# The top-4 choice of a mixture of experts moved into the attention ahead of it, with the experts' up weights loaded during that attention's last quads

## The reference, cut to what matters

```python
H, NH, NOPE, ROPE, VD, E, I, TOPK = 256, 16, 128, 64, 128, 16, 176, 4
SHI = I * 2
hid = hidden_states + attn_out
x2 = rmsnorm(hid, ln2_w).reshape(-1, h)
logits = x2 @ gate_w.T
probs = jax.nn.softmax(logits, axis=-1)
top_w, top_i = jax.lax.top_k(probs, TOPK)
top_w = top_w / jnp.sum(top_w, axis=-1, keepdims=True)
gu = jnp.einsum('th,eih->tei', x2, w1)          # g, u = its two halves
act = jax.nn.silu(g) * u
down = jnp.einsum('tei,ehi->teh', act, w2)
routed = jnp.einsum('te,teh->th', wfull, down)  # wfull: top_w at the chosen experts
shared = jax.nn.silu(sg) * su @ sh_down_w.T     # sg, su = halves of x2 @ sh_gu_w.T
return hid + (routed + shared).reshape(b, s, h)
```

## Time and profile before

| what | value |
|---|---|
| runs | 2027.96, 2036.36, 2041.23 us; median 2036.36 |
| profiled execution | 2040.3 us, its span 2038.6 us |
| TensorE busy | 1617.7 us (79%) |
| VectorE busy | 1374.7 us (67%) |
| ScalarE busy | 819.6 us (40%) |
| GpSimd busy | 600.5 us (29%) |
| mean granted TensorE clock | 0.901 of full |

### The profile page before, as it was taken

The page is one execution under the profiler, slowest core; times in us unless marked ns, Lnnn a source line. Parts: engine busy times, 40 slices in busy tenths (PEclk is TensorE's granted clock), DMA queues, the critical chain, the costliest instruction groups (busy, mean ns, idle before and its releaser), DMA issues. The chain is left out here.

```text
span 2038.6 us, 29782 instructions
## 1 busy us (share of the span) xinstructions
PE 1617.7 (79%) x9318; PEld 1137.7 (56%) x9318; DVE 1374.7 (67%) x3796; ACT 819.6 (40%) x2363; POOL 600.5 (29%) x720
## 2 busy tenths in 40 slices
PE   3559998788253888889889499999954999698883
PEld 2424443355121566666666388888842555588872
DVE  6679969588794888888888435555355333368875
ACT  2113444376231666666667223333310222144551
POOL 0020002167303877787777210000025000311000
PEclk9679999889576999999999799999966999799996
DMA  1305520100665600000000500000062222523100
GB/s 62 109 0 172 184 88 1 66 13 1 28 133 199 212 1 1 2 1 1 1 1 1 175 23 1 15 1 1 1 205 85 76 89 76 209 94 106 60 32 11
DMA packets 104406, 129.33 MB, mean 63 GB/s; under 512 B 14208, under 2 KB 89185, under 8 KB 101057
## 3 DMA queue, kind: packets, MB, share of 16 engines
q1 hardware_dynamic: 95264, 112.39, 17.2%
q0 software_dynamic: 8992, 15.08, 3.6%
HBM read 85.75 MB, written 46.94 MB: 65 GB/s over the span
## 5 line engine op out<-in xcount | busy, mean ns | idle before, releaser
L580 POOL TENSOR_TENSOR l0f_diag<-g_identb,l0f_mask 128x1024 bf16<-128x1024 bf16 x16 | 32.0, 2024 | 227.7 <-PE l0f_psA L836 208.8
L2773 ACT ACTIVATE l2x_probs<-l2x_psS,l2x_nmax 128x128 f32<-128x128 f32 x256 | 90.8, 373 | 10.6 <-DVE l2x_nmax L2687 10.5
L2557 POOL TENSOR_TENSOR l2x_probs<-l2x_probs,l2x_rtotal 128x512 f32<-128x512 f32 x64 | 66.9, 1045 | 93.3 <-DVE l2x_rtotal L2693 93.3
L3260 DVE COPY moe_xgT<-moe_psX 128x256 f32<-128x256 f32 x47 | 19.9, 424 | 103.0 <-PE moe_psX L3369 103.0
L2568 POOL TENSOR_TENSOR l2x_vsm<-l2x_vraw,l2x_smooth_row 128x512 f32<-128x512 f32 x64 | 84.6, 1343 | 4.8 <-ACT l2x_vraw L2807 4.6
L3125 POOL MEMSET moe_before<- 128x256 f32 x1 | 0.3, 317 | 287.2 <-POOLq L162 287.2
L3437 POOL DMA_INDIRECT routed_rows<-rows,slots_slot_of x32 | 31.5, 983 | 169.8 <-DMA rows<-moe_yg 161.1
L2918 PEld LDWEIGHTS l2x_psS<-l2x_kT,l2x_qT 128*128 128x128 f32 x512 | 66.8, 191 | 22.3 <-issue 17.9
L819 PE MATMUL l0f_psH<-l0f_wT,l0f_xm 128*128 128x512 bf16 x256 | 68.2, 390 | 9.7 <-DVE l0f_h L660 9.0
L3362 PE MATMUL moe_psG<-moe_w,moe_xgT 128*128 x188 | 70.5, 499 | 4.9 <-issue 1.6
L1040 ACT ACTIVATE l1a_probs<-l1a_psS,l1a_nmax 128x256 f32<-128x256 f32 x128 | 58.9, 472 | 38.0 <-PE l1a_psT L1068 25.6
(11 more groups left out here) (540 smaller groups left out, 4892.1 us busy)
## 6 DMA issues: line engine op xcount, KB each, us to landing
rows<-l2x_zero SPq DMA_DIRECT2D x1, 18304.0 KB, 59.8
kT_ctx<-l0f_held SPq DMA_DIRECT2D x32, 256.0 KB, 3.5
v_ctx<-l0f_held SPq DMA_DIRECT2D x32, 256.0 KB, 3.6
l3a_kT<-kT_ctx SPq DMA_DIRECT2D x8, 1024.0 KB, 6.5
l3a_v<-v_ctx SPq DMA_DIRECT2D x8, 1024.0 KB, 6.3
l0f_wrow<-in_L_ffn_w SPq DMA_DIRECT2D x24, 256.0 KB, 3.0
moe_xg<-rows SPq DMA_DIRECT2D x47, 128.0 KB, 2.0
rows<-moe_yg SPq DMA_DIRECT2D x47, 128.0 KB, 1.7
```

The source lines that it names most:

```text
L2557: nc.gpsimd.tensor_tensor(probs[:, n % 2, :, :], probs[:, n % 2, :, :], rtotal[:, n % 2, :].unsqueeze(2).to_broadcast([P, 4, P]), ALU.mult)\
L2773: last = nc.scalar.activation(probs[:, n % 2, j, :], psS[:, j, :], ACT.Exp, bias=nmax[:, n % 2, j:j + 1], scale=1.0, accum_out=total[:, n ...
```

## The change

A class `Router` holds the choice for one sample at a time, cut into eight steps, each in a slot that counts from the quad after the sample's attention is done: variance, rows (the normed tokens), turn, logits, compare, choose, count and assign, weigh. Samples 0 to 6 go through these steps in the attention's slots, sample 6 only up to its logits; the rest of sample 6 and all of sample 7 are done in the first units of `moe_16`. TensorE's part writes into the bank `psO`, so `wait_bank` lets the values wait until VectorE has read it: three waits a sample. GpSimd adds the attention's result to x sample by sample and scatters samples 0 to 5 during the attention. The attention's three projections now lie in one tile, `home`; when the last sample is projected (`v_done`), SyncE loads into their place one half of the shared up weights and all of w1. `AHEAD` goes from 8 to 10 half units, so 6 are left behind the tiles. The compares work on one sample (256 elements) where they worked on two (512).

```diff
+        columns = KC * NH * HD
+        wq, wk, wv = (home[:, j * columns:(j + 1) * columns].rearrange("p (c o) -> p c o", c=KC) for j in range(3))
...
+class Router:
...
+    VARIANCE, ROWS, TURN, LOGITS, COMPARE, CHOOSE, COUNT, WEIGH = 3, 4, 5, 7, 8, 9, 11, 12
...
+    def scatter(self, pool, G, s):
+        pool.wait_ge(self.placed, s + 1)
+        for k in range(TOP2):
+            n = s * TOP2 + k
+            self.nc.gpsimd.indirect_dma_start(G.rows, bass.IndirectOffsetOnAxis(ap=self.slot_of[:, n:n + 1], axis=0),
+                                              G.ctx[:, s, :], None).then_inc(self.scattered, 16)
+    def add_hid(self, pool, G, s):
+        self.nc.gpsimd.tensor_tensor(G.x[:, s, :], G.x[:, s, :], self.hid[:, s, :], ALU.add).then_inc(self.hid_added, 1)
...
+        dve.wait_ge(self.rrms_ready, s + 1)
+        self.nc.vector.scalar_tensor_tensor(out=G.ctx[:, s, :], in0=self.hid[:, s, :], scalar=self.rrms[:, :],
+                                            in1=self.lnw[:, :], op0=ALU.mult, op1=ALU.mult).then_inc(self.x2_ready, 1)
...
+    def turn(self, pe, G, s):
+        pe.wait_ge(self.x2_ready, s + 1)
+        wait(pe, self.count_taken, s)
+        for c in range(KC):
+            last = self.nc.tensor.transpose(self.psT[:, c, :], G.ctx[:, s, c * P:(c + 1) * P], G.ident[:, :])
+        last.then_inc(self.turned, 1)
...
+        dve.wait_ge(self.turned, s + 1)
+        self.nc.vector.tensor_copy(G.ctxT[:, :, s, :], self.psT).then_inc(self.x2T_ready, 1)
...
+        pe.wait_ge(self.x2T_ready, s + 1)
+        for c in range(KC):
+            last = self.nc.tensor.matmul(self.psL, G.ctxT[:, c, s, :], self.gate[:, c, :], start=(c == 0), stop=(c == KC - 1))
+        last.then_inc(self.logits_ready, 1)
...
+        dve.wait_ge(self.logits_ready, s + 1)
+        self.nc.vector.tensor_copy(self.scores[:, :], self.psL).then_inc(self.logits_taken, 1)
+        dve.wait_ge(self.logits_taken, s + 1)
+        self.nc.vector.tensor_reduce(self.nmax[:, :], self.scores[:, :], AX.X, ALU.max, negate=True).then_inc(self.max_ready, 1)
...
+        o.mark(nc.vector.tensor_tensor(self.gt, other, own, ALU.is_gt))
+        o.step(nc.vector.tensor_tensor(self.eq, other, own, ALU.is_equal))
+        o.step(nc.vector.tensor_tensor(self.eq, self.eq, self.before[:, :, :], ALU.mult))
+        o.step(nc.vector.tensor_tensor(self.gt, self.gt, self.eq, ALU.add))
...
+    def count(self, pe, G, s):
+        pe.wait_ge(self.chosen_ready, s + 1)
+        nc = self.nc
+        nc.tensor.matmul(self.psP, self.above[:, :], self.chosen[:, :], start=True, stop=False)
+        last = nc.tensor.matmul(self.psP, G.ones[:, :], self.earlier[:, s % 2, :], start=False, stop=True)
...
+    def in_slot(self, h, step):
+        s, rest = divmod(h - step, 8)
+        return s - 1 if rest == 0 and 1 <= s < B else None
+    def on_vector(self, dve, G, h):
+        s = self.in_slot(h, self.WEIGH)
+        if s is not None:
+            self.weigh(dve, s)
+        s = self.in_slot(h, self.COUNT)
+        if s is not None:
+            self.assign(dve, s)
+        s = self.in_slot(h, self.TURN)
+        if s is not None:
+            self.copy_turned(dve, G, s)
+        s = self.in_slot(h, self.LOGITS)
+        if s is not None:
+            self.maximum(dve, s)
+        s = self.in_slot(h, self.COMPARE)
+        if s is not None:
+            self.compare(dve, s)
+        s = self.in_slot(h, self.CHOOSE)
+        if s is not None:
+            self.choose(dve, s)
+        s = self.in_slot(h, self.ROWS)
+        if s is not None:
+            self.rows(dve, G, s)
+        s = self.in_slot(h, self.VARIANCE)
+        if s is not None:
+            self.variance(dve, s)
...
+    def wait_bank(self, pe, h):
+        for step, taken in ((self.TURN, self.x2T_ready), (self.LOGITS, self.logits_taken), (self.COUNT, self.count_taken)):
+            s = self.in_slot(h, step)
+            if s is not None:
+                pe.wait_ge(taken, s + 1)
...
+    def on_gpsimd(self, pool, G, added):
+        self.constants(pool, G)
+        for s in range(B - 1):
+            self.invert(pool, G, s)
+            self.add_hid(pool, G, s)
+            if s > 0:
+                self.scatter(pool, G, s - 1)
...
+        for c in range(KC):
+            sp.dma_start(self.shared[:, c, :].rearrange("p (s i) -> p s i", s=2), shared[c * P:(c + 1) * P, 0, :, :])\
+                .then_inc(self.shared_loaded, 16)
+        for c in range(KC):
+            sp.dma_start(self.w1[:, c, :, :], A["L2f_w1T"][c * P:(c + 1) * P, :, :]).then_inc(self.w1_loaded, 16)
...
+        self.prep.on_sync(sp, G, A)
+        sp.wait_ge(self.v_done, NH // 4 * B)
+        self.W2.load(sp, A)
...
+    def on_vector(self, dve, G, h, added):
+        if h == self.routes.LOGITS + 8:
+            dve.wait_ge(self.prep.hots_ready, 5)
+        self.routes.on_vector(dve, G, h)
...
-        GROUP = 2
-        GROUPS = B // GROUP
-        AHEAD = 2 * 4
-        STEP = AHEAD // GROUPS
+        AHEAD = 2 * 5
...
-        w1 = T.sb("w1", [P, KC, E2, 2 * I2])
+        w1 = W2.w1
...
-                for c in range(KC):
-                    sp.dma_start(w1[:, c, :, :], A["L2f_w1T"][c * P:(c + 1) * P, :, :]).then_inc(w_loaded, 16)
...
-                nc.gpsimd.tensor_tensor(G.x[:, :, :], G.x[:, :, :], hid[:, :, :], ALU.add).then_inc(made, 1)
...
+                pool.wait_ge(made, MADE)
+                routes.scatter(pool, G, B - 2)
+                routes.add_hid(pool, G, B - 1)
+                routes.scatter(pool, G, B - 1)
...
                 def route(m):
-                    g, j = divmod(m, STEP)
-                    if j == 0:
-                        if g > 0:
-                            assign(g - 1)
-                        if g < GROUPS:
-                            compare(g)
-                            break_ties(g)
-                        else:
-                            list_tiles()
-                    elif g < GROUPS:
-                        choose(g)
+                    s = B - 1
+                    if m == 0:
+                        routes.variance(dve, s)
+                        routes.compare(dve, s - 1)
+                        routes.choose(dve, s - 1)
+                        routes.rows(dve, G, s)
+                        routes.assign(dve, s - 1)
+                        routes.weigh(dve, s - 1)
+                    elif m == 1:
+                        routes.copy_turned(dve, G, s)
+                    elif m == 2:
+                        routes.maximum(dve, s)
+                    elif m == 3:
+                        routes.compare(dve, s)
+                    elif m == 4:
+                        routes.choose(dve, s)
+                    elif m == 5:
+                        routes.assign(dve, s)
+                        list_tiles()
+                    elif m == 6:
+                        routes.weigh(dve, s)
...
+                    if m == 1:
+                        pe.wait_ge(shared_loaded, 16 * KC)
                     for c in range(KC):
                         if i is None:
-                            x, w = x2T[:, c, (n // 2) * P:(n // 2 + 1) * P], shw[:, c, n % 2, :]
+                            x, w = G.ctxT[:, c, n // 2, :], (W2.shared, shw)[n % 2][:, c, :]
...
+                    if m == 0:
+                        routes.turn(pe, G, B - 1)
+                    if m == 1:
+                        routes.logits(pe, G, B - 1)
+                    if m == 4:
+                        routes.count(pe, G, B - 1)
```

412 lines of the change are left out of this document (231 added, 181 removed).

## The result

The changed kernel takes 2008.7 us (median of 4 runs, 2005.06 to 2010.24) where the kernel before takes 2036.4; the ratio is 0.9866, its 95% interval 0.983 to 0.990. The forecast was 2005, in a range from 1991 to 2024. The profiled execution has a span of 2006.4 us against 2038.6, 32.2 less.

| stretch | before | after | forecast |
|---|---|---|---|
| start of the span to the attention's first projection | 1161.0 | 1155.6 (-5.4) | 0 |
| from there to `moe`'s first operation (S) | 327.9 | 349.7 (+21.8) | +16.8 |
| S to the first tile's up product | 84.2 | 41.9 (-42.3) | -38 |
| first tile to layer 3's first projection | 178.2 | 168.6 (-9.6) | -9.5 |
| from there to the end | 287.3 | 290.6 (+3.3) | 0 |

What follows compares the result with a forecast made beforehand. TensorE was taken to bound the attention and tiles, waits at a low clock the start of moe. -38 - 4.2 - 5.3 + 16.8 = -30.7 us from a median of 2036.4 gave a forecast of 2005, range 1991 to 2024.

Steps and rivals of the forecast that it cites:

- The start of `moe`: First operation to first tile: 46 us for 84.2, so -38, including a 6.3 us listing wait and 4.2 of cold clock.
- Tiles and tail: Behind the start of moe: first tiles warm, -4.2 us; two half units fewer in the tail, -5.3 us.
- TensorE's own work in the attention: Seven turns at 0.21 us, seven logits at 0.44 and six counts at 0.33 add 6.6 us.
- the prediction's own sign: In the attention: if quads without roundings grow by over half a microsecond, hand-overs bind, not VectorE's load.
- VectorE's lag: Attention: lag beyond the free one adds 1.8 us at quad 8, 1.2 at 15, 4.2 at 20 to 22, together 7.2.
- The last quads: End of the attention: the last four quads depend on latency, and sample 6's steps in them add 1 us.
- GpSimd's adds: In the attention: seven adds may hold VectorE's two-input operations, 3.9 us at most; 2.0 us taken.
- At nothing: Late attention: early w1 load, 15.1 us, has some 27 us of cover; ScalarE's small operations and GpSimd's scatters also cost nothing.
- The slow start: Rival at the start of moe: TensorE never warm, first tile at S + 60, total 2024 us; chance 14%.
- the better case: Rival: TensorE warm through the units, first tile at S + 39, attention lag free, total 1992 us; chance 10%.
- Each bank wait stops TensorE: Rival in the attention: 20 bank waits at 1 us in place of 7.2, total 2018 us; chance 12%.
- The slower case: Rival in the attention: TensorE waits through each sample's hand-overs and is cold after, 76 us for 16.8, total 2064; chance 6%.

Runs made afterwards that it cites:

- e_list3: Changed kernel with the 16 listing operations split in three, behind the sixth, seventh and eighth half unit; 2004.4 us, 0.9853 of the kernel before.
- e_spread: Changed kernel with layer 3's roundings spread over every second slot and their consumers moved later too; 2001.1 us, 0.9834 of the kernel before.
- e_round45: Changed kernel with the last rounding of layer 3's down weights moved from slot 44 to slot 45; 2011.6 us, 0.9878 of the kernel before.
- e_double: Changed kernel with the first pass of each compare in the attention (samples 0 to 5) made five times; 2023.1 us, 0.9919 of the kernel before.
- e_shift: Changed kernel with compare, choice and weights one slot later (steps 9, 10 and 13); 2012.7 us, 0.9871 of the kernel before.
- e_add1col: Changed kernel with GpSimd's seven adds in the attention taking one column of 256, the rest of the sum left out; 2014.3 us in one run.
- e_w1_late: Changed kernel with w1 and half of the shared weights loaded at the start of moe, not in the attention; 2012.0 us, 0.9897 of the kernel before.
- b_all: Changed kernel with the edits of e_spread and e_list3, and the first half unit's up product ahead of sample 6's count; 1991.5 us, 0.9777.

## Why the prediction was right

Its mechanism was right: most of the old start of `moe` went, and VectorE's lag at the places named took part of it back. That the sum is as near as it is (-42.3 + 21.8 - 9.6 = -30.1 against -30.7) is luck: the start of `moe` came out 4.3 us better and the attention 5.0 us worse, and the first of these varies by 2 us from trace to trace.

**The start of `moe`.** The first shared product stood at S + 4.3 (4.7 forecast). The first two half units took 6.1 us instead of 8.0: TensorE was warm by the third. The listing's wait was 4.5 for 6.3, and the slow clock behind it about 3, for 4.2 (the unit periods 5.13 and 3.33, taken from one unit's first transpose to the next one's, stand where 2.66 is usual). With the 0.4 of the start these are 5.3 us, of which 4.1 show; the rest is small and of the other sign. e_list3 shows that wait and clock go together: 6.3 to 6.8 us of them came back.

**Tiles and tail.** -9.6 for -9.5. The first tiles were warm, and two half units fewer stood behind them. Other traces of the same code have -7.5 to -9.3 here, so the agreement to 0.1 is chance.

**TensorE's own work in the attention.** A turn cost 0.51 to 0.55 (0.22 where no tokens of the attention are turned beside it), logits 0.40, a count 0.29: 3.1 + 2.8 + 1.7 = 7.6 us, for 6.6. The turn was the one mis-sized: I had taken the price of a pair of transposes of before, 0.21, and it is that only where it stands alone. By the prediction's own sign (quads without roundings that grow by over half a microsecond) the hand-overs should bind there; no wait stands in these quads, and the products account for the growth.

**VectorE's lag.** Forecast 1.8, 1.2 and 4.2 us at quads 8 and 9, 15, and 20 to 22; measured 3.2, 0.95 and 6.9. The places were right, the size 11.1 for 7.2. What was missing at the last is the clock: I priced waits, and not that the work behind a wait of 3.6 us is slow (2.4 us here). e_spread, which takes most of the lag away and leaves all the routing in, gives 10.1 us back, part of it lag that the kernel before had too. e_round45 shows that moving one copy ahead of a rounding is not enough: its consumer then waits.

**The last quads** were mis-sized most by factor: 2.9 us for 1.0. TensorE waits for VectorE in each of them, so whatever VectorE does there lies on the path; e_double shows it there, 3.6 us for 1.7 added, and e_shift, which gets 1.7 us back by moving three steps one slot on. Here the sign of being wrong was right: the periods 27 to 28 and 29 to 30 grew by 1.2 and 1.8 us without a rounding in them, and it is the hand-overs that bind.

**GpSimd's adds** were given 2.0 us; e_add1col finds nothing to within 0.2. GpSimd does hold VectorE up: beside an add a pass of the rounding (L1587) took 0.94 us, and 0.53 in e_add1col. That pass has only one tensor as its input, where the prediction reckoned with operations of two inputs. It stands in one of seven places, and VectorE had the time.

**At nothing** stood the early load of w1. Its loads started at 1470.6, later than the prediction's 1460, and had landed 15.9 us before S. It is nothing in both directions: e_w1_late shows that the load in `moe` would have done as well, since with the choice gone from there the first tile is still 42 us behind S. In e_list3 and b_all the first tile comes at S + 34, and with the late load its rows landed only at S + 38.5; so they should need the early load, by some 4 us, but the two were not tried together.

**The rivals.** The slow start (first tile at S + 60) didn't come, nor the better case. "Each bank wait stops TensorE" is refuted: at the logits and counts of most samples the period grows by the products alone (0.40, 0.29) and the profile has no wait. The slower case, a wait of TensorE with slow work behind it, came true in one place of the changed kernel, the period 21 to 22.

VectorE's share was sized well: from the attention's first projection to S its routing instructions take 39.2 us, 6.3 for each of the six samples whose choice ends there, against 6.5 forecast (seven samples, 45 us, were reckoned, but only the first steps of sample 6 stand there). It is busy for 194.1 us of this stage, where it was busy for 157.5. The time lost hangs on where the work stands, not on how much it is: e_spread has as much of it and loses 10.1 us less.
